# Two-layer relational graph attention on one core: which engine copies the turned W1 tiles of the pair loop out of PSUM

## The chip, the cores and the metric

The kernel runs on one core of one Trainium2 chip. The metric is the device time of one execution in microseconds (us), lower is better; a kernel's time is the median of its runs. The engines of the core work side by side, each through its own list of instructions, and meet only at semaphores: PE (TensorE, the matmuls), DVE (VectorE), ACT (ScalarE), POOL (GpSimd) and SP (SyncE, which here issues nearly all transfers).

## The reference, cut to what matters

There are 1250 nodes with 768 features and 40000 edges (source, destination, one of 3 relations). Two layers of relational graph attention follow each other, and a residual with a layer normalisation ends it:

```python
def rgat_conv(x, W, q, k, b, src, dst, etype, heads, out_ch, n_nodes):
    xr = jnp.einsum('nd,rdf->rnf', x, W)
    oi = xr[etype, dst]
    oj = xr[etype, src]
    alpha = jax.nn.leaky_relu(oi @ q + oj @ k, 0.2)
    m = jax.ops.segment_max(alpha, dst, num_segments=n_nodes)
    e = jnp.exp(alpha - m[dst])
    z = jax.ops.segment_sum(e, dst, num_segments=n_nodes)
    a = e / (z[dst] + 1e-16)
    msg = (a[:, :, None] * oj.reshape(-1, heads, out_ch)).reshape(-1, heads * out_ch)
    return jax.ops.segment_sum(msg, dst, num_segments=n_nodes) + b
h = jax.nn.elu(rgat_conv(x, W1, q1, k1, b1, ...))      # 4 heads of 192
y = rgat_conv(h, W2, q2, k2, b2, ...)                  # 1 head of 768
out = layernorm(x + y)
```

All that the change touches belongs to the first layer. There the kernel computes W1 times q1 and W1 times k1 ahead of time (so that the attention terms come out of the same matmul as x times W1), and for that it needs each 128-row tile of W1 turned.

## The kernel before, in words

**The stages.** The work begins with the edges: they are packed into codes, sorted by destination already, and gathered into windows of 6 destination nodes. From these the kernel builds `Ct`, a matrix of edge counts (source by relation and destination). The build is the **pair loop**: 106 pairs of windows. For each pair PE makes four bf16 matmuls of one-hot matrices (L1036) into PSUM bank 0 or 1, in turn; ACT copies the bank to `Ct` as 16-bit integers (L689). The one-hot matrices of two pairs, a **quad**, are made by DVE in two comparisons (L1265), one for the sources (128x1024) and one for relation and window (128x1440). There are 53 quads and two buffers, so quad q may be built only when pair 2q-3 has left PE, and pairs 2q and 2q+1 need it.

PE and ACT are tied by the two PSUM banks: pair p waits for the copy of pair p-2 (`c_ready`), and the copy of pair p waits for its matmuls (`c_done`).

**W1 inside the pair loop.** W1 has 3 relations of 6 row tiles, 18 tiles. The first 10 are handled ahead of the loop. The other 8 (tile i = 10 to 17) are put between the pairs by the table `WT_AT = {0: 10, 3: 11, 6: 12, ..., 21: 17}`: after the matmuls of pair p PE turns the tile with six transposes (L913) into two PSUM banks (`wt_tr`). The two banks are then copied, 128x384 fp32 each, to the buffer `WT[i % 2]` in SBUF, in `wt_out` (L639, on ACT; `wt_ready`). Three pairs later (`WQ_AT = {3: 10, 6: 11, ..., 24: 17}`) PE multiplies the copied tile with q1 and k1 (`wq_product`, L930, `wq_done`). In ACT's list `wt_out` of the tile turned at pair p stands behind the copy of pair p+1. At the end of a relation ACT copies the products to SBUF (`wq_out`, L623), and PE then turns and sums them (L942); within the loop this happens for relation 1 around pairs 6 to 12 and for relation 2 at pairs 24 and 25. The load of a later W1 slot (`load_w` on SP, L435) and POOL's four small memsets wait for `wq_done` too.

**After pair 27** the product x times W1, first half (L959), is put between the pairs in small portions; the loop ends with pair 105. Behind it PE goes on with L959, while ACT makes masks and DVE walks through the segment maxima (L1319). Then follow the attention of layer 1 (L1132 on PE, L1376 and L1380 on DVE), the product with W2 (L984) and the attention of layer 2 (L1174).

The order of the work on each engine is written out in its own function, and the loops over pairs (L686 on ACT, L1029 on PE) and quads (L1257 on DVE) advance side by side only through the semaphores named.

Of the kernel before, what the change touches and what calls it, by code (L numbers as in the profile page):

```python
# [36 lines left out]
def rgat(nc, x, src, dst, etype, W1, q1, k1, b1, W2, q2, k2, b2, out):  # L37
# [15 lines left out]
    HF = F // 2  # L53
# [38 lines left out]
    with ExitStack() as ctx:  # L92
# [3 lines left out]
        def sem(name):  # L96
            return ctx.enter_context(nc.semaphore(name))
# [42 lines left out]
        ps = [ctx.enter_context(nc.psum_tensor(f"ps{i}", [P, 512], F32)) for i in range(8)]  # L140
# [52 lines left out]
        WT = [bb[:, i * F:(i + 1) * F] for i in range(2)]  # L193
# [95 lines left out]
        S = {n: sem(n) for n in names}  # L289
# [45 lines left out]
        WT_AT = {3 * (i - PRE): i for i in range(PRE, R * KT)}  # L335
# [8 lines left out]
        def steps0(pair):  # L344

            n = PAIRS - T_AT
            return range(max(0, NK0 * (pair - T_AT) // n), max(0, NK0 * (pair + 1 - T_AT) // n))
# [27 lines left out]
        def wt_bank(i):  # L375

            return 4 if i % 2 == 0 else 2
# [232 lines left out]
        def _(act):  # L610
# [6 lines left out]
            def wq_out(i):  # L617

                r, kt = i // KT, i % KT
                if kt == KT - 1:  # L620
                    act.wait_ge(S["wq_done"], i + 1)
                    for b in range(2):
                        last = nc.scalar.activation(wqs[0:QP, b * HF:(b + 1) * HF], ps[6 + b][0:QP, 0:HF], copy)  # L623
                    last.then_inc(S["wqs_ready"], 1)
                if kt == 1 and r:
                    wq_columns(r - 1)

            def wq_columns(r):
                act.wait_ge(S["wq_tr"], r + 1)
                o = wqk1.rearrange("p k (a r h) -> p r k a h", a=2, r=R)[:, r]  # L630
                nc.scalar.activation(o, ps[7][:, HF:HF + KT * 2 * H].rearrange("p (k a h) -> p k a h", k=KT, a=2), copy).then_inc(S["wq_ready"], 1)

            def wt_out(i):

                act.wait_ge(S["wt_tr"], i + 1)
                if i >= 2:
                    act.wait_ge(S["wq_done"], i - 1)
                for b in range(2):
                    last = nc.scalar.activation(WT[i % 2][:, b * HF:(b + 1) * HF], ps[wt_bank(i) + b][:, 0:HF], copy)  # L639
                last.then_inc(S["wt_ready"], 1)  # L640

            def transform_out(u):
                b, t = UNITS1[u]
                if u == 0:
                    act.wait_ge(S["ones_in"], NS1)
                act.wait_ge(S["t_done"], u + 1)
                if u >= NS1:
                    act.wait_ge(xr_out[u % NS1], 16 * (u // NS1))
                o = stg1[u % NS1].rearrange("p (h c) -> p h c", h=2)[:, :, 0:HD]
                v = unit1_bank(u)  # L650
                if b == 0:
                    nc.scalar.activation(qk1t[:, t, :], v[:, HF:HF + QC], copy)
                    nc.scalar.activation(ks1[:, t, :], v[:, HF + QC // 2:HF + QC], copy, scale=SLOPE).then_inc(S["qk_ready"], 1)
                nc.scalar.activation(o, v[:, 0:HF].rearrange("p (h c) -> p h c", h=2), copy).then_inc(S["t_evac"], 1)  # L654
# [31 lines left out]
            for pair in range(PAIRS):  # L686
                act.wait_ge(S["c_done"], pair + 3)
                d = 2 * pair * WIN
                nc.scalar.activation(Ct[:, :, d:d + 2 * WIN].rearrange("p a (c b) -> p a c b", c=2),  # L689
                                     ps[pair % 2][:, 0:2 * WM].rearrange("p (c a b) -> p a c b", c=2, b=WIN), copy).then_inc(S["c_ready"], 1)  # L690
                if pair - 1 in WT_AT:
                    wt_out(WT_AT[pair - 1])
                if pair - 1 in WQ_AT:
                    wq_out(WQ_AT[pair - 1])
                if pair - 1 == WQ_END:
                    wq_columns(R - 1)
                for n in steps0(pair - 1):
                    if n % KT == KT - 1:
                        transform_out(n // KT)
# [22 lines left out]
            for _, kind, i in sorted(events):  # L722
                if kind == 0 and i >= U1 - 2:
                    if i == U1 - 2:
                        act.wait_ge(ab_in[0], 16)
                    exp_step(0, 0, i - U1 + 2)
                if kind == 0 and i == AB1_AT:
                    ab_rows(L1)
                (mask1 if kind else transform_out)(i)
# [452 lines left out]
        def _(dve):  # L1182
            V = nc.vector
            links = [0]

            def link(ins):

                links[0] += 1
                ins.then_inc(S["chain"], 1)
                dve.wait_ge(S["chain"], links[0])  # L1190
# [61 lines left out]
            for o, v in ((slo_2, slo), (mcode_2, mcode)):  # L1252
                for a in range(2):
                    last = V.tensor_copy(o[:, :, a].rearrange("p (s w t) -> p s t w", s=2, t=RUN), v.rearrange("p (s t w) -> p s t w", s=2, t=RUN))
                link(last)

            for quad in range(QUADS):  # L1257
                h, col = quad % 2, quad * 4 * RUN
                if quad >= 2:
                    dve.wait_ge(S["c_done"], 2 * quad)  # L1260
                if quad == 2:
                    dve.wait_ge(S["flag_tot"], 1)
                    V.tensor_copy(smalli[0:1, 4:5], ps[6][0:1, 511:512]).then_inc(S["flag_ready"], 1)
                for o, w, iota, codes in ((oh_s, P, i_s, slo_2), (ohm_s, WM, i_m, mcode_2)):
                    last = V.tensor_tensor(o[:, h * 4 * RUN:(h + 1) * 4 * RUN, :].rearrange("p n (b a) -> p n b a", a=2),  # L1265
                                           iota[:, :].rearrange("p (b a) -> p b a", a=2).unsqueeze(1).broadcast_to([P, 4 * RUN, w // 2, 2]),
                                           codes[:, col:col + 4 * RUN, :].unsqueeze(2).broadcast_to([P, 4 * RUN, w // 2, 2]), ALU.is_equal)
                last.then_inc(S["oh"], 1)
# [3 lines left out]
            with dve.If(held < E):  # L1272
# [7 lines left out]
                with dve.Fori(0, NW) as w:  # L1280
# [10 lines left out]
                    with dve.Fori(0, EC // 4) as j:  # L1291
                        dve.wait_ge(S["fb_c"], w * 5 + 5)
                        dve.wait_ge(S["fb_used"], w * (EC // 4) + j + 1)
                        for t in range(4):
                            V.tensor_scalar(ohs[t][0:EP, :], i_s[0:EP, :], slo_[0:EP, bass.ds(j * 4 + t, 1)], None, ALU.is_equal)
                            last = V.tensor_scalar(ohm[t][0:EP, :], i_m[0:EP, :], 1.0, mcode_[0:EP, bass.ds(j * 4 + t, 1)], ALU.add, ALU.is_equal)
# [206 lines left out]
            i = 0  # L1503
# [116 lines left out]
```

## Time and profile before

| | us |
|---|---|
| median of 3 runs (lowest 1292.36, highest 1293.78) | 1293.2 |
| the profiled execution | 1294.57 |
| its span, first to last instruction | 1292.6 |
| PE busy in the span | 1249.7 |
| DVE busy | 989.4 |
| ACT busy | 757.7 |
| pairs 0 to 25 with the eight W1 tiles, about | 41 to 66 |
| end of the pair loop, about | 138 |

Busy times say how long an engine had an instruction in work, not that it was at its peak. Where the text says that an engine waited, the profile has named the event that ended the wait. A number in brackets, as [rows 2], is a group of rows in the section below.

### The profile page before, as it was taken

How to read it: one execution, taken by the hardware profiler on the slowest of the kernel's cores; microseconds unless marked ns; L12 is line 12 of the kernel's file. 1: busy time of each engine (PE TensorE's matmuls, PEld its weight loads, DVE VectorE, ACT ScalarE, POOL GpSimd, SP SyncE). 2: the span in 40 equal slices, each digit the busy share in tenths (PEclk: the TensorE clock that was granted, in tenths of full speed). 3: DMA queues.
4: the chain of work that ended last, by engine and by line, in shares of the span. 5: the costliest groups of instructions: out<-in, count | busy, mean ns of one | idle time of the engine just before them, and what ended most of it. 6: DMA issues, size and time to landing. Idle time of an engine off the chain costs nothing.

```text
span 1292.6 us, 18743 instructions
## 1 busy us (share of the span) xinstructions
PE 1249.7 (97%) x7104; PEld 1121.7 (87%) x7104; DVE 989.4 (77%) x1289; ACT 757.7 (59%) x1210; POOL 4.9 (0%) x20
## 2 busy tenths in 40 slices
PE   6899999999999999999999999999989999999996
PEld 4766656665699999999999999999989999999995
DVE  4678899999399899999989967759844466656554
ACT  4655432332499889979979942257434444464462
POOL 1000000000000000000000000000000000000000
PEclk9999999999999999999999999999989999999998
DMA  9420131111553333323313237944486776778860
GB/s 314 164 92 31 44 122 49 50 50 43 194 122 103 103 96 103 96 68 116 118 50 99 64 109 236 313 160 159 159 307 235 248 246 204 264 261 305 283 230 34
DMA packets 93847, 195.32 MB, mean 151 GB/s; under 512 B 16125, under 2 KB 66366, under 8 KB 93762
## 3 DMA queue, kind: packets, MB, share of 16 engines
q1 hardware_dynamic: 93568, 193.77, 45.1%
q8 instruction: 57, 0.93, 0.3%
q0 software_dynamic: 96, 0.23, 0.1%
q14 instruction: 28, 0.23, 0.1%
q10 hardware_dynamic: 98, 0.16, 0.0%
HBM read 154.28 MB, written 39.85 MB: 150 GB/s over the span
## 4 chain that ended last, share of the span: by engine, by line
PE 76%; DVE 13%; ACT 4%; DMA 3%; issue 3%; SPq 1%; PEld 1%; ACTq 0%; DVEq 0%
PE ps L1174 24%; PE ps L1132 24%; PE ps L959 13%; PE ps L984 10%; DMA arena<-in_L_gnn_W 3%; DVE arena L1319 3%; PE ps L1036 3%; DVE arena L1376 2%; DVE arena L1380 2%; ACT arena L718 1%; ACT arena L719 1%; DVE ps L1448 1%; DVE misc L1329 1%; DVE arena L1461 1%; DVE arena L1398 1%
## 5 line engine op out<-in xcount | busy, mean ns | idle before, releaser
L1132 PE MATMUL ps<-arena 128*128 128x193 f32 x2400 | 396.9, 327 | 1.8 <-DVE arena L1380 1.5
L1132 PEld LDWEIGHTS ps<-arena 128*128 128x128 f32 x2400 | 392.1, 190 | 4.3 <-DVE arena L1380 3.8
L959 PE MATMUL ps<-arena,xT 128*128 128x384 f32 (+1 forms) x720 | 249.6, 494 | 0.0
L718 ACT ACTIVATE arena<-arena,misc 128x640 f32<-128x640 f32 x240 | 196.9, 820 | 31.5 <-DVE arena L1376 23.7
L959 PEld LDWEIGHTS ps<-arena,xT 128*128 128x128 f32 x720 | 131.4, 191 | 76.4 <-issue 0.3
L719 ACT ACTIVATE arena<-arena,misc 128x640 f32<-128x640 f32 x240 | 195.7, 815 | 0.0
L1376 DVE TENSOR_TENSOR arena<-arena 128x1280 f32<-128x1280 f32 x120 | 178.4, 1486 | 20.9 <-ACT arena L719 20.8
L1380 DVE SCALAR_TENSOR_TENSOR arena<-arena,Ct 128x1280 f32<-128x1280 f32 x120 | 179.2, 1493 | 15.0 <-DVE arena L1376 11.0
L1319 DVE SCALAR_TENSOR_TENSOR arena<-arena,misc 128x1250 f32<-128x1250 bf16 x108 | 155.8, 1520 | 1.5 <-ACT arena L663 1.5
L835 ACT ACTIVATE g_hi<-arena 128x512 fp32r<-128x512 f32 (+2 forms) x90 | 49.7, 552 | 158.8 <-PE ps L1174 143.6
L1174 PE MATMUL ps<-x2a,g_hi 128*128 128x384 f32 (+1 forms) x600 | 131.8, 342 | 5.2 <-issue 5.2
L1174 PE MATMUL ps<-x2b,g_hi 128*128 128x384 f32 (+1 forms) x600 | 130.2, 338 | 1.8 <-DVE g_lo L1480 1.8
L984 PE MATMUL ps<-w_hi,xt_hi 128*128 128x384 f32 (+1 forms) x360 | 122.1, 339 | 1.3 <-DVE w_lo L1427 1.3
L984 PE MATMUL ps<-w_lo,xt_hi 128*128 128x384 f32 (+1 forms) x360 | 121.4, 337 | 0.0
L984 PE MATMUL ps<-w_hi,xt_lo 128*128 128x384 f32 (+1 forms) x360 | 121.3, 337 | 0.0
L1480 DVE TENSOR_TENSOR g_lo<-arena,g_hi 128x512 fp32r<-128x512 f32 (+2 forms) x90 | 53.3, 592 | 82.4 <-ACT g_hi L835 82.1
L1174 PEld LDWEIGHTS ps<-x2a,g_hi 128*128 128x128 f32 (+1 forms) x600 | 108.3, 189 | 6.2 <-issue 5.5
L654 ACT ACTIVATE bb<-ps 128x384 f32<-128x384 f32 x60 | 29.6, 494 | 142.2 <-PE ps L959 141.2
L1174 PEld LDWEIGHTS ps<-x2b,g_hi 128*128 128x128 f32 (+1 forms) x600 | 106.5, 186 | 3.2 <-DVE g_lo L1480 2.5
L1265 DVE TENSOR_TENSOR arena<-misc,arena 128x1024 bf16<-128x1024 bf16 x106 | 78.0, 794 | 18.7 <-PE ps L1036 18.4
L793 ACT ACTIVATE stg<-ps 128x384 fp32r<-128x384 f32 x60 | 29.3, 489 | 94.5 <-PE ps L984 85.7
L1469 DVE TENSOR_TENSOR arena<-arena 128x512 f32<-128x512 f32 (+2 forms) x90 | 53.1, 590 | 40.0 <-ACT arena L828 39.9
(174 smaller groups left out, 1356.8 us busy)
## 6 DMA issues: line engine op xcount, KB each, us to landing
x2a<-xr_d SPq DMA_DIRECT2D x45, 776.0 KB, 4.3
x2b<-xr_d SPq DMA_DIRECT2D x45, 776.0 KB, 4.5
arena<-xr_d SPq DMA_DIRECT2D x120, 193.0 KB, 2.4
xr_d<-stg SPq DMA_DIRECT2D x60, 384.0 KB, 3.0
arena<-ab_d SPq DMA_DIRECT2D x12, 1280.0 KB, 6.4
xr_d<-bb SPq DMA_DIRECT2D x60, 193.0 KB, 2.2
arena<-in_L_gnn_W SPq DMA_DIRECT2D x5, 2304.0 KB, 9.8
arena<-in_L_gnn_W SPq DMA_DIRECT2D x7, 1152.0 KB, 6.8
```

What stands on the lines that cost most here:

```text
L718: nc.scalar.activation(weights1(g, r, t)[:, h, :], abr[:, r, h, :], ACT.Exp, bias=qk1t[:, t, col + R * H:col + R * H + 1])
L719: last = nc.scalar.activation(e2[t % 2][:, h, :], abr[:, r, 2 + h, :], ACT.Exp, bias=ks1[:, t, col:col + 1])
L959: last = mm(unit1_bank(u)[:, 0:w], xT[:, kt, t * P:(t + 1) * P], v, start=kt == 0, stop=kt == KT - 1)
L984: last = mm(unit_bank(u)[:, 0:w], a[:, t, kt, :], v[b % 2][:, kt, 0:w], start=kt == 0 and n == 0, stop=kt == KT - 1 and n == 2)
L1132: last = mm(bank1(g, i)[:, o:o + HD + 1], weights1(g, r, t)[:, h, i * P:(i + 1) * P], xring[t % NX][:, o:o + HD + 1], start=False, stop=Tr ...
L1174: last = mm(banks[b][0:k, 0:wide], a, xs[:, x0 + b * HF:x0 + b * HF + wide], start=j == 0 and m == 0, stop=j == RS - 1 and m == 2)
L1265: last = V.tensor_tensor(o[:, h * 4 * RUN:(h + 1) * 4 * RUN, :].rearrange("p n (b a) -> p n b a", a=2), iota[:, :].rearrange("p (b a) -> p ...
L1319: last = V.scalar_tensor_tensor(m[:, h, 0:N], cneg[i % NCN][:, 0:N], k, m[:, h, 0:N], ALU.min, ALU.max)
L1376: V.tensor_tensor(a, a, e2[t % 2], ALU.max).then_inc(S["e2_free"], 1)
L1380: V.scalar_tensor_tensor(a, a, 1.0, cc.broadcast_to([P, 2, DH]), ALU.min, ALU.mult).then_inc(S["a_ready"], 1)
L1469: link(V.tensor_tensor(v, v, g2[n % 2][:, 0:w], ALU.max))
L1480: V.tensor_tensor(g_lo[n % NG][:, 0:w], g1[n % NG][:, 0:w], g_hi[n % NG][:, 0:w], ALU.subtract).then_inc(S["a_ready"], 1)
```

## The change

The eight copies of turned W1 tiles that stand inside the pair loop leave ACT's list and go to DVE's. ACT's own copies of the ten tiles ahead of the loop stay. On DVE a tile is copied by two `tensor_copy` of 128x384 fp32, at the head of the turn of quad q, for the tile turned at pair 2q-4 or 2q-3: ahead of quads 2, 3, 5, 6, 8, 9, 11 and 12. Ahead of the copy DVE waits until the tile is turned (`wt_tr`), until the buffer's last product is done (`wq_done`) and until the tile before is there (`wt_ready`). The one-hot matrices of the quad are built behind it. Nothing else is edited.

```diff
@@ scalar: the pair loop
                 nc.scalar.activation(Ct[:, :, d:d + 2 * WIN]...).then_inc(S["c_ready"], 1)
-                if pair - 1 in WT_AT:
-                    wt_out(WT_AT[pair - 1])
                 if pair - 1 in WQ_AT:
                     wq_out(WQ_AT[pair - 1])
@@ vector: ahead of the quads
+            def wt_copy(i):
+
+                dve.wait_ge(S["wt_tr"], i + 1)
+                dve.wait_ge(S["wq_done"], i - 1)
+                dve.wait_ge(S["wt_ready"], i)
+                for b in range(2):
+                    last = V.tensor_copy(WT[i % 2][:, b * HF:(b + 1) * HF], ps[wt_bank(i) + b][:, 0:HF])
+                last.then_inc(S["wt_ready"], 1)
+
             for quad in range(QUADS):
                 h, col = quad % 2, quad * 4 * RUN
+                for p in (2 * quad - 4, 2 * quad - 3):
+                    if p in WT_AT:
+                        wt_copy(WT_AT[p])
                 if quad >= 2:
                     dve.wait_ge(S["c_done"], 2 * quad)
```

## Rows read from the trace of the kernel before

**Rows 1.** Two stretches: length, busy us by engine; last: granted clock, DMA share, GB/s

```profile
40.00:66.00 26.00, 22.76 (x287) 17.22 (x286) 17.90 (x26) 17.36 (x46) 0.20 (x4) 1.00 0.26 94
...
70.20:73.60 3.40, 3.40 (x12) 1.77 (x11) 2.12 (x3) 0.85 (x2) 0.00 (x0) 0.51 0.88 353
```

**Rows 2.** Chain of waits, pair 18 until pair 21: start us, us, what

```profile
58.60 0.47 PE ps L1036 x4
59.08 0.66 PE ps L913 x6
59.73 0.55 PE ps L930 x12
60.28 0.43 PE ps L1036 x4
60.71 0.02 issue
60.73 0.48 ACT Ct L689
61.21 0.14 issue
```

**Rows 3.** Timeline of DVE, first quads of the loop: start us, us, idle before

```profile
42.65 0.15 DVE L1263 CAST smalli<-ps 1x1 uint32<-1x1 f32 x1 [5.02 <-PE ps L1040]
42.73 4.33 DVE L1265 TENSOR_TENSOR arena<-misc,arena 128x1024 bf16<-128x1024 bf16 x6
...
51.46 1.51 DVE L1265 TENSOR_TENSOR arena<-misc,arena 128x1024 bf16<-128x1024 bf16 x2 [0.57 <-PE ps L1036]
```

**Rows 4.** Chain of waits, tile 10 turned behind pair 0, and pair 6

```profile
41.45 0.66 PE ps L913 x6
...
45.82 0.47 PE ps L1036 x4
```

**Rows 5.** Groups of instructions, for the price of a copy: busy us, mean ns | idle us before

```profile
L1239 DVE CAST arena<-ps 128x424 int32<-128x424 f32 x1 | 0.6, 600 | 11.6 <-PE ps L1019 11.6
L1229 DVE CAST arena<-arena 128x424 f32<-128x424 int32 x1 | 0.4, 381 | 0.0
L1398 DVE SCALAR_TENSOR_TENSOR arena<-ps,small,bb 128x192 f32<-128x192 f32 x40 | 13.4, 409 | 0.1
L1329 DVE TENSOR_REDUCE misc<-ps 128x4 f32<-128x512 f32 x30 | 18.9, 686 | 0.8 <-PE ps L1074 0.8
```

**Rows 6.** Timeline: a tile's ACT copies, two stalls of L930, a W1 load

```profile
48.32 0.87 ACT L639 ACTIVATE bb<-ps 128x384 f32<-128x384 f32 x2
...
50.07 0.62 PE L930 MATMUL ps<-bb,misc 128*8 128x128 f32 x12 [0.37 <-ACT arena L623]
...
64.77 0.62 PE L930 MATMUL ps<-bb,misc 128*8 128x128 f32 x12 [0.20 <-ACT bb L639]
65.44 0.37 SPq L435 DMA_DIRECT2D arena<-in_L_gnn_W  x1
```

**Rows 7.** Timeline of PE: pairs 9 and 12

```profile
48.57 0.48 PE L1036 MATMUL ps<-arena 128*128 128x180 bf16 x4 [0.34 <-ACT Ct L689]
...
51.76 0.48 PE L1036 MATMUL ps<-arena 128*128 128x180 bf16 x4 [0.34 <-ACT Ct L689]
```

**Rows 8.** Chain of waits, after pair 28, at half and at full clock

```profile
70.08 1.23 PE ps L959 x2
71.30 0.60 PE ps L1036 x4
71.90 1.43 PE ps L959 x2
...
75.88 0.31 PE ps L1036 x4
76.19 0.72 PE ps L959 x2
```

**Rows 9.** Chain of waits, behind the pair loop

```profile
138.32 70.38 PE ps L959 x218
```

## The prediction, made before the changed kernel ran

> **What bounds the kernel now.** I read the slices of the page first (PE is full nearly everywhere from pair 28 on), then the busy times of the stretch in which the eight tiles are handled, then the chain of waits through it, and last the timeline of DVE and PE there. From 40 to 66 us no engine is full: in 26 us PE is busy 22.8, DVE 17.9, ACT 17.4 [rows 1]. This is a loop of dependences, not of a full engine. The chain shows its beat, which takes three pairs: pair 18's matmuls 0.47, six transposes 0.66, the product L930 0.55, pair 19's matmuls 0.43, then ACT's copy of pair 19 with 0.02 ahead and 0.14 behind it, 0.64 together, and pair 21 follows: 2.75 us [rows 2]. The ACT copies of the tile (L639) are not in this beat. They stand behind the copy that PE waits for, and the product that needs them comes three pairs later. They are seen in the chain only where they push something else: L930 waits 0.37 us for ACT's L623, which stands behind a tile copy, and once 0.20 us for a tile copy itself [rows 6].
>
> DVE is near its limit in another way. It has room in the mean, but each quad has a start (pair 2q-3 has left PE) and a due time (pair 2q). For quads 2, 3 and 4 it runs without a gap from 42.73 for 4.33 us [rows 3]: quad 2 ends at 42.73 + 1.51 = 44.24 and quad 3, at (4.33 - 1.51)/2 = 1.41 more, at 45.65, while pair 6, the first that needs quad 3, starts at 45.82 [rows 4]. From the end of a quad to the pair that waits for it are thus at most 0.17 us. I take 0.13 for the signal. Whatever is put ahead of quad 3 lands on PE nearly in full.
>
> **The copy on DVE.** The trace has no 128x384 copy from PSUM on DVE. A cast of 128x424 from PSUM took 600 ns, one of the same size from SBUF 381 ns [rows 5]. The first is 424 columns at 0.96 GHz, 442 ns, and 158 ns fixed; the second goes at twice that pace. So 384 columns from PSUM would be 400 + 158 = 558 ns. Back to back an instruction hides a part of its duration: the 40 instructions of L1398 have a mean of 409 ns but 13.4/40 = 335 ns busy each [rows 5], 74 ns less. A tile then holds DVE for 2 x 0.484 = 0.97 us. Bounds: if a plain copy from PSUM ran as the cast from SBUF did, 381 less 40/1.92 = 360 ns, 0.29 held, 0.57 a tile. The longest row for a like amount of PSUM data is the reduction of 128x512, 686 ns [rows 5]; 0.61 held, 1.22 a tile. I take 0.97, because the PSUM cast is the same kind of operation with the same source.
>
> The Trainium skill, VectorE: DVE Perf Modes, section on the TRN2 errata, gives a copy from PSUM to SBUF 120 cycles beside its elements. By that a copy would hold DVE 504/0.96 = 525 ns, an estimate, and four tiles on the path would cost 4 x 2 x 0.04 = 0.3 us more than the sum below. No copy of this kind is in the trace; L1398, with two operands more, shows 335 ns for 192 columns where that rule would make it 325.
>
> **The first two tiles.** Tile 10 is turned at 41.45 + 0.66 = 42.11 [rows 4]. DVE, idle until 42.65 now [rows 3], copies it from 42.13 to 43.10, makes the small cast (it shifts the next by 0.08) and quad 2 from 43.18 to 44.69; pair 4 is due at 44.75 and is late by 0.07 at most. Tile 11 is turned behind pair 3 (45.82 - 2.75 = 43.07, + 0.47 + 0.66 = 44.20), so DVE need not wait for it: copy 44.6 to 45.6, quad 3 until 47.07, pair 6 at 47.20 in place of 45.82. That is **+1.38 us**.
>
> **The steady beat.** Of the remaining six tiles, three (12, 14, 16) are turned at pairs 6, 12 and 18, which is pair 2q-4 of the quad that they precede, and three (13, 15, 17) at pairs 9, 15 and 21, which is pair 2q-3. For the second kind the copy can't be early: its transposes are the last thing ahead of the quad. The path from pair p to pair p+3 is then: matmuls 0.47, transposes 0.66, signal 0.02, two copies 0.97, the quad 1.51, signal 0.13, together 3.76 us, where the beat is 2.75 now. That is **+1.0** each, for tiles 15 and 17. For the first kind the quad is ready in time: copies begin 1.15 behind pair 2q-4, the quad ends at 1.15 + 0.97 + 1.51 = 3.63, and pair 2q would come at 2.75 + 0.47 + 0.66 + 0.55 = 4.43. So no cost. But DVE may still be at the quad without a tile that stands between; after a late pair 6 it makes quad 4 until 47.07 + 1.43 = 48.50, and tile 12 is turned at 47.20 + 1.13 = 48.33. It costs 0.2 out of the 0.8 of slack. The whole load says the same: three quads of 1.45 and two tiles are 6.3 us, just under the 6.5 us which two beats take then.
>
> **What comes back.** Tile 13's beat (pair 9 to pair 12) takes 51.76 - 48.57 = 3.19 us now [rows 7], because L930 waits for L623. With the tile copy off ACT, L623 begins 0.87 us earlier [rows 6] and ends ahead of the transposes. So this beat goes from 3.19 to 3.76, **+0.57**. At pair 24 the tile has long been there, and the wait of 0.20 goes [rows 6]; the product itself takes 0.62 when it starts from idle [rows 6] and 0.55 in the chain when it doesn't [rows 2], so I count **-0.25**. The third thing freed is ACT's time, 8 x 0.87 = 7.0 us, and nothing in this stretch waits for ACT except through the copy at 0.64, which stays as long as it is.
>
> The sum: 1.38 + 0.57 + 1.0 + 1.0 - 0.25 = **+3.7 us** at pair 27.
>
> **Behind it.** From pair 28 on PE is full, and from 138.32 a single piece of the chain is 70.38 us of L959 [rows 9]. DVE's maxima, which end the stage later, begin with the end of the same loop. Neither has an origin other than the pair loop, so the delay goes through in full. The load of a later W1 slot, issued at 65.44 now [rows 6] behind `wq_done`, moves by the same 3.7 us; it is of a W1 slot that L959 reads only behind 138, so it is hidden, as are POOL's memsets. SP and POOL are moved past nothing. In DVE's list behind each `wt_copy` are its quad and all later quads, and PE waits for those; that is the cost counted. If L959 had slack anywhere up to 272 us, it would be hidden; its row shows none.
>
> The profiled span would be 1292.6 + 3.7 = 1296.3. The profiled execution is 1.4 above the median of the runs; the difference is laid on the median: 1293.2 + 3.7 = **1296.9 us**. With the copy at 0.57 the late starts are 0.60, 0.6 - 0.44, 0.6, 0.6 and -0.25, +1.7: 1294.9. With 1.22 four tiles cost 0.25 each more, +4.7: 1297.9.
>
> **Rivals.**
>
> *A longer stretch at half clock.* From 70.2 to 73.6 the granted clock is 0.51, that is the 1.2 GHz level, behind the idle time at pairs 25 to 27; around it is full [rows 1]. It costs: two portions of L959 take 1.23 and 1.43 where they take 0.72, and four pair matmuls 0.60 in place of 0.31 [rows 8], 1.22 + 0.29 = 1.5 us. The change adds waits of PE of about 1 us ahead of pairs 6, 12, 18 and 24, the last just ahead of the idle time that there is. A second stretch of this kind makes +3.7 + 1.5 = +5.2: 1298.4. Against it: one such stretch is all that 40 to 74 us shows now, with waits of 0.34 in each beat. The Trainium skill, TensorE: Matmul & The Clock Gate, Part 1, says that activity releases the throttle and an idle array falls back to it. By that rule the trace agrees: the low level at 70.2 follows the longest idle time of PE in this stretch.
>
> *DVE absorbs the copies and ACT's relief is what remains.* This is the rival on the other side. DVE is idle 8.1 of the 26 us [rows 1] and the copies are 7.8. If the copies fell into those gaps, PE would gain 0.37 + 0.25: 1292.6, not slower. It decides on whether the idle time lies ahead of a tile's copy or behind it. For tiles 12, 14 and 16 it fits, for 11, 13, 15 and 17 the gap lies ahead of transposes that have not run.
>
> *The delay is given back later.* 3.7 us of delay at pair 27 vanish in a wait that was there anyway, for instance DVE's maxima against the masks of ACT at 272 us: 1293.2, unchanged. Against it, all of them count from the end of the pair loop.
>
> *The cheap copy*, at SBUF pace, 1294.9 as above; under 0.2% from before.
>
> **How the numbers follow.** Forecast (with copies between 0.8 and 1.22) 0.55, own range 1295.6 to 1298.0; longer half clock 0.23; cheap copy 0.09; given back 0.07; ACT's relief 0.06. A measurement tells 0.2%, 2.6 us, from no change: slower means above 1295.8. Slower: 0.53 of the forecast and 0.23, 0.76. Same: 0.02 + 0.09 + 0.07 and 0.02 of the relief, 0.20. Faster: 0.04. The range takes in the cheap copy and a half-clock stretch over a dear copy's half: 1294.6 to 1299.6.
>
> **What would show it.** Right: two DVE copies per tile of about 560 ns with source PSUM; pair 6 at about 47.2 us in the span; PE waiting for DVE's L1265 about 1 us ahead of pairs 6, 12, 18 and 24 and nowhere else by that much; DVE waiting for L913 ahead of tiles 13, 15 and 17; no wait of L930 for ACT; the end of the loop 3.7 us later and the distance from there to the end unchanged. Wrong: copies near 360 ns; waits of PE ahead of the other quads too, which would mean DVE is full; a second stretch at a granted clock of about 0.5 between 40 and 80; or a later stage shorter than before.

## The result, and the profile after

The changed kernel takes 1297.04 us (median of 7 runs, 1295.42 to 1298.74), the kernel before 1293.78 (7 runs beside it, 1292.36 to 1294.09). The ratio is 1.003 with a 95% interval of 1.0018 to 1.0041: slower by 2.3 to 5.3 us. The medians are 3.26 apart, with 3.7 forecast.

The stretch in which the eight tiles are handled, in the same window as in [rows 1]. Columns: length, busy us of PE, PEld, DVE, ACT and POOL with the number of instructions, granted clock, DMA share, GB/s.

```profile
40.00:66.00 26.00, 20.00 (x241) 15.38 (x239) 23.18 (x39) 11.27 (x27) 0.00 (x0) 1.00 0.25 94
```

DVE has gone from 17.9 to 23.2 of 26 us, ACT from 17.4 to 11.3, and PE has fallen from 22.8 to 20.0. Less of PE's work fits into the same time. Who waits for whom there (us in all, times, longest), for PE:

```profile
PE ps L1034 <- DVE arena L1275: 5.3, 4, 1.6
PE ps L1034 <- ACT Ct L689: 1.0, 3, 0.3
```

L1034 and L1275 are the L1036 and L1265 of before. The list of PE's matmuls shows where the four waits are (start, us, line, idle before and what ended it). The rows are pairs 4 and 5, 6, 9, 12, 15, 18, 21, 24 and 25; [rows 4 and 7] have pairs 6, 9 and 12 of before.

```profile
43.47 0.80 PE L1034 MATMUL ps<-arena 128*128 128x180 bf16 x8
45.82 0.49 PE L1034 MATMUL ps<-arena 128*128 128x180 bf16 x4 [1.55 <-DVE arena L1275]
...
48.58 0.48 PE L1034 MATMUL ps<-arena 128*128 128x180 bf16 x4 [0.34 <-ACT Ct L689]
...
52.25 0.49 PE L1034 MATMUL ps<-arena 128*128 128x180 bf16 x4 [1.25 <-DVE arena L1275]
...
56.35 0.48 PE L1034 MATMUL ps<-arena 128*128 128x180 bf16 x4 [0.34 <-ACT Ct L689]
...
60.02 0.49 PE L1034 MATMUL ps<-arena 128*128 128x180 bf16 x4 [1.25 <-DVE arena L1275]
...
62.78 0.48 PE L1034 MATMUL ps<-arena 128*128 128x180 bf16 x4 [0.34 <-ACT Ct L689]
...
66.45 0.49 PE L1034 MATMUL ps<-arena 128*128 128x180 bf16 x4 [1.25 <-DVE arena L1275]
...
67.42 0.49 PE L1034 MATMUL ps<-arena 128*128 128x180 bf16 x4
```

A beat without a DVE wait takes 2.76 us (62.78 - 60.02), as before; one with it 3.67 us (66.45 - 62.78). Every second beat is long. The chain of waits shows what fills a long one, pair 21 to pair 24, beside the short one of [rows 2]:

```profile
62.78 0.48 PE ps L1034 x4
63.26 0.67 PE ps L911 x6
63.92 0.02 issue
63.95 1.02 DVE bb L1261 x2
64.97 1.43 DVE arena L1275 x2
66.40 0.05 issue
66.45 0.49 PE ps L1034 x4
```

Matmuls, transposes, two copies, two one-hot matrices, one behind the other: neither the product L928 nor ACT's copy is on the path any more. DVE's own list shows that it waited for the transposes and not they for it, and what a copy costs:

```profile
61.30 1.01 DVE L1261 COPY bb<-ps 128x384 f32<-128x384 f32 x2
62.23 1.50 DVE L1275 TENSOR_TENSOR arena<-misc,arena 128x1024 bf16<-128x1024 bf16 x2
63.95 1.02 DVE L1261 COPY bb<-ps 128x384 f32<-128x384 f32 x2 [0.22 <-PE ps L911]
64.89 4.57 DVE L1275 TENSOR_TENSOR arena<-misc,arena 128x1024 bf16<-128x1024 bf16 x6
```

A copy lasts 549 ns in the median of the 16, and a tile shifts what follows it by 0.93 or 0.94 us (63.95 to 64.89).

**Where the time went**, counted from pair 0 so that all that runs ahead of the loop drops out:

| us after pair 0 | before | after | difference |
|---|---|---|---|
| pair 6 | 4.85 | 6.09 | +1.24 |
| pair 9 | 7.60 | 8.85 | +1.25 |
| pair 12 | 10.79 | 12.52 | +1.73 |
| pair 15 | 14.88 | 16.62 | +1.74 |
| pair 18 | 17.63 | 20.29 | +2.66 |
| pair 24 | 23.13 | 26.72 | +3.59 |
| pair 25 | 24.35 | 27.69 | +3.34 |
| end of the pair loop | 97.35 | 100.35 | +3.00 |

From there to the end are 1154.3 us before and 1154.4 after. The end of the loop is +3.00 and not +3.34 because a stretch at half clock behind pair 26 costs a little less in the profile of after than in that of before; two later profiles without such a stretch (the kernels filled with zeros, below) end the loop at 95.69 and 99.00, 3.31 apart. The profiled span itself grew by only 1.9 (1292.6 to 1294.5), because pair 0 stands at 39.73 in place of 40.97, and the clock goes with this difference. Two stretches of both kernels, before first:

```profile
33.00:37.00 4.00, 3.89 (x30) 3.58 (x30) 3.93 (x8) 1.74 (x4) 0.00 (x0) 0.62 1.03 397
...
66.00:76.00 10.00, 8.55 (x52) 5.88 (x53) 5.49 (x8) 4.24 (x11) 0.00 (x0) 0.83 0.67 236
```

```profile
33.00:37.00 4.00, 3.69 (x45) 2.89 (x46) 3.93 (x7) 2.51 (x6) 0.00 (x0) 1.00 1.03 396
66.00:76.00 10.00, 8.06 (x58) 5.61 (x59) 6.31 (x9) 3.97 (x10) 0.20 (x4) 0.83 0.65 236
```

The profiled execution of before ran a part of 33 to 37 us at the 1.2 GHz level, that of after did not. Of the eleven profiles here only this one and one other (odd tiles behind, below) show it; their pair 0 stands at 40.97 and 40.94, that of the nine others at 39.45 to 40.05. Nothing ahead of pair 0 was edited, so a comparison of the two spans would have made the change look 1.2 us cheaper than it is.

### The profile page after: what moved, and what is told of

It is laid out like the page before. It is cut to its first block, busy times and chain, and to the rows that moved or that the text cites. A ratio compares the mean times of both kernels' runs of the same rounds, so it can differ in the third digit from the quotient of the medians.

```text
span 1294.5 us, 18743 instructions
## 1 busy us (share of the span) xinstructions
PE 1246.4 (96%) x7104; PEld 1118.7 (86%) x7104; DVE 996.7 (77%) x1305; ACT 752.2 (58%) x1194; POOL 4.9 (0%) x20
## 4 chain that ended last, share of the span: by engine, by line
PE 75%; DVE 14%; ACT 4%; DMA 3%; issue 3%; SPq 1%; PEld 1%; ACTq 0%; DVEq 0%
PE ps L1172 24%; PE ps L1130 23%; PE ps L957 13%; PE ps L982 10%; DMA arena<-in_L_gnn_W 3%; DVE arena L1329 3%; PE ps L1034 2%; DVE arena L1386 2%; DVE arena L1390 2%; ACT arena L716 1%; ACT arena L717 1%; DVE ps L1458 1%; DVE misc L1339 1%; DVE arena L1471 1%; DVE arena L1408 1%
## 5 line engine op out<-in xcount | busy, mean ns | idle before, releaser
L654 ACT ACTIVATE bb<-ps 128x384 f32<-128x384 f32 x60 | 29.6, 494 | 142.4 <-PE ps L957 141.1
L1275 DVE TENSOR_TENSOR arena<-misc,arena 128x1024 bf16<-128x1024 bf16 x106 | 78.0, 794 | 14.2 <-PE ps L1034 14.1
```

## The experiments

The first measure of each is the start of pair 25 after the start of pair 0 in the profile: before 24.35, after 27.69. I had written some expectations for pair 28; where the clock falls between them pair 25 is the clean one, and what was expected for pair 28 is compared by its difference from before. At pair 28 itself the first four experiments stand at 28.83, 32.64, 31.13 and 29.79 us, where 28.5, 31.5, 29.6 and 29.7 were expected; in the first three the half clock begins ahead of pair 28, and in the fourth just at it. Edits are shown against the changed kernel unless said otherwise, and the ratio is always to the runs of the kernel before in the same batch.

**Only the even tiles on DVE** (the ones turned at pair 2q-4).

```diff
+                if i >= PRE:
+                    act.wait_ge(S["wt_ready"], i)
...
+                if pair - 1 in WT_AT and WT_AT[pair - 1] % 2 != 0:
+                    wt_out(WT_AT[pair - 1])
...
-                    if p in WT_AT:
+                    if p in WT_AT and WT_AT[p] % 2 == 0:
                         wt_copy(WT_AT[p])
```

The first two lines stand in `wt_out`: with two engines copying in turn, ACT too waits until the tile before is there.

> Tiles 10, 12, 14 and 16 are copied by VectorE, tiles 11, 13, 15 and 17 by ScalarE. Measured in the profile from the first matmul of pair 0 to the first of pair 28: 28.63 us before, 31.97 us with all eight on VectorE (+3.34). Theory A (the cost is a path: only the tile turned at pair 2q-3 pays, because its transposes are the last thing ahead of the quad): tile 10 delays quads 2 and 3 by 0.43, which pair 6 feels as +0.3; tiles 12, 14 and 16 cost nothing; the wait of L930 for L623 goes (-0.44); so -0.1, 28.5 us, and no wait of PE for L1275 above 0.1 us but the one ahead of pair 6 (about 0.3 beyond the wait for ScalarE). Theory B (VectorE's time is what is paid, evenly over the tiles, 3.34/8 = 0.42 each): +1.7, 30.3 us. Theory C (relief of ScalarE counts): below 28.0.

Measured: pair 6 at 5.15 (+0.30), pair 25 at 24.23 (-0.12). The time is 1292.15 us, ratio 1.000 (0.999 to 1.0009). Four tiles on DVE cost nothing net (+0.30 at pair 6, -0.44 at pair 12); the only wait for DVE is the one ahead of pair 6:

```profile
PE ps L1038 <- ACT Ct L691: 2.0, 6, 0.3
PE ps L944 <- ACT arena L623: 1.3, 1, 1.3
PE ps L1038 <- DVE arena L1279: 0.6, 1, 0.6
PE ps L932 <- ACT bb L641: 0.2, 1, 0.2
```

The lines L1038, L1279, L944 and L932 are the L1036, L1265, L942 and L930 of before. The wait of the product for L623 is gone. At pair 25 theory A holds to 0.02 us, and B is out.

**Only the odd tiles on DVE.** The same edit with `% 2 != 1` on ACT and `% 2 == 1` on DVE.

> The other half: tiles 11, 13, 15 and 17 on VectorE, 10, 12, 14 and 16 on ScalarE. Theory A: +0.8 at pair 6 (the 1.24 of the changed kernel less the 0.43 that tile 10 gave), +0.48 from pair 9 to pair 12, +0.92 from 15 to 18 and from 21 to 24, -0.25 at pair 25: +2.9, 31.5 us from pair 0 to pair 28, though VectorE has only half of the copies. Theory B: +1.7, 30.3 us.

Measured: pair 6 +0.92, pair 12 +1.40, pair 25 at 27.36 (+3.01); 1296.17 us, ratio 1.0027 (1.0017 to 1.0037). The same number of copies on the same engine as in the run before, and nearly the whole cost of the change:

```profile
PE ps L1038 <- DVE arena L1279: 4.6, 4, 1.3
PE ps L1038 <- ACT Ct L691: 1.0, 3, 0.3
PE ps L932 <- ACT arena L623: 0.4, 1, 0.4
```

It matters which tile is copied there, more than how many. The two halves add up to 2.89 and not to 3.34: with tile 13 on DVE the beat from pair 9 to pair 12 waits for DVE, and the 0.44 that the even tiles alone gave back there is not had.

**All eight on DVE, the odd ones behind their quad.** The position alone is changed, the instructions are those of the changed kernel.

```diff
                 for p in (2 * quad - 4, 2 * quad - 3):
-                    if p in WT_AT:
+                    if p in WT_AT and WT_AT[p] % 2 == 0:
                         wt_copy(WT_AT[p])
...
                 last.then_inc(S["oh"], 1)
+                if 2 * quad - 3 in WT_AT:
+                    wt_copy(WT_AT[2 * quad - 3])
```

> All eight tiles on VectorE as in the changed kernel, same instructions, but the tiles turned at pair 2q-3 (11, 13, 15, 17) are copied behind the one-hot matrices of quad q, not ahead of them. Theory A with VectorE's load as the floor: the path over the transposes is cut; worked through by the same durations, pair 6 +0.3, pair 12 +0.5, pair 24 +0.3, and at pair 24 the product waits about 0.4 for tile 17; in all about +1.0, 29.6 us from pair 0 to pair 28. Theory B (the load alone decides): the load is the same, so +3.3, 32.0 us.

Measured: pair 6 at 5.15, pair 12 at 11.27 (+0.48), pair 24 at 23.87 (+0.74), pair 25 at 25.35 (+1.00); 1294.18 us, ratio 1.0012 (1.0002 to 1.0022). Of 3.34 us 2.34 were the position, so theory B is out here too. What is left is DVE's load and one late product:

```profile
PE ps L1034 <- DVE arena L1275: 1.7, 4, 0.6
PE ps L1034 <- ACT Ct L689: 1.5, 4, 0.6
PE ps L928 <- DVE bb L1261: 0.4, 1, 0.4
```

Pair 24 stands at +0.74 where I had written +0.3: the 0.3 was what is added there, on top of pair 12's shift. The list of waits puts 0.59 us ahead of pair 24 to ACT, but DVE's list has two quads from 61.83 for 2.92 us, so until 64.75, and pair 24 starts at 64.81:

```profile
61.83 2.92 DVE L1275 TENSOR_TENSOR arena<-misc,arena 128x1024 bf16<-128x1024 bf16 x4
64.67 1.02 DVE L1261 COPY bb<-ps 128x384 f32<-128x384 f32 x2
```

```profile
64.81 0.49 PE L1034 MATMUL ps<-arena 128*128 128x180 bf16 x4 [0.59 <-ACT Ct L689]
```

It is DVE's load that is the floor here, as the forecast of the run has it: from 42.13 us until pair 24 has started, DVE waits once, for 0.27 us ahead of 55.70.

**Each tile half by ACT, half by DVE.** ACT copies the first 384 columns at its old place, with a semaphore of its own for PE.

```diff
+                if pair - 1 in WT_AT:
+                    i = WT_AT[pair - 1]
...
+                    nc.scalar.activation(WT[i % 2][:, 0:HF], ps[wt_bank(i)][:, 0:HF], copy).then_inc(S["wt_half"], 1)
...
-                for b in range(2):
+                for b in range(1, 2):
                     last = V.tensor_copy(WT[i % 2]...)
```

> Each of the eight tiles is copied half by VectorE (second 384 columns) and half by ScalarE (first 384 columns), each where its copy of a whole tile stood. Theory A (the path holds the copies in series): one copy less on the path, 0.46 to 0.47 us, so pair p to pair p+3 takes 3.21 in place of 3.67: +0.35 at pair 6, 0.0 from 9 to 12, +0.46 from 15 to 18 and from 21 to 24, -0.25 at pair 25: +1.0, 29.7 us. Theory D (a wait of PE for VectorE costs a fixed price by itself, whatever is copied): the steps stay near 3.67, about +3 in all.

Measured: pair 6 +0.45, pair 9 +0.47, pair 12 +0.48, pair 25 at 25.50 (+1.15); the long beats take 3.19 to 3.20 us in place of 3.67. 1293.92 us, ratio 1.0005 (0.9995 to 1.0015). One copy less shortens the path by 0.47 to 0.48, its own share; pair 6 was 0.1 dearer than I had said. Theory D is out. The lines L1043, L1284 and L949 are the L1036, L1265 and L942 of before.

```profile
PE ps L1043 <- DVE arena L1284: 3.1, 4, 0.8
PE ps L1043 <- ACT Ct L689: 1.4, 4, 0.3
PE ps L949 <- ACT arena L623: 1.3, 1, 1.3
```

**ACT's relief alone.** In the kernel without DVE copies ACT copies 8 columns of each tile at the old place. The kernel leaves out the rest of each copy, so the products read mostly old data, and its time alone is of use.

```diff
+                    nc.scalar.activation(WT[i % 2][:, 0:8], ps[wt_bank(i)][:, 0:8], copy).then_inc(S["wt_ready"], 1)
...
-                for p in (2 * quad - 4, 2 * quad - 3):
-                    if p in WT_AT:
-                        wt_copy(WT_AT[p])
```

> ScalarE's relief without VectorE's copies. The eight tiles are not copied: in place of each ScalarE copies 8 columns at the same place in its list, so that the products in the loop read mostly old data (work left out, time only). Theory A: PE waited for ScalarE's tile copies only at the product of tile 12 (0.37 and 0.07 of restart) and of tile 17 (0.20 and 0.05), so pair 25 starts 0.7 us after pair 0 earlier than before, at 23.7 in place of 24.35, and the time falls by 0.7, hardly to be told. Theory C (ScalarE is what the stretch turns on): each of the eight beats gets shorter by some of the 0.87 us of a tile copy, 2 to 6 us in all.

Measured: pair 25 at 23.65, so 0.70 us is all that ACT's relief can bring up to there, and theory C is out. The time was 1292.79 us, ratio 0.9994 (0.9983 to 1.0005), with its runs 6.7 us apart.

**The clock: the kernel before, with PE kept busy in two waits.** The edit is against the kernel before.

```diff
                 elif kt == 0:
+                    if r == 1:
+                        for _ in range(6):
+                            mm(ps[5][:, 0:512], zm[:, 0:P], zm[:, 0:512], start=True, stop=True)
                     pe.wait_ge(*landed(r))
...
                 if pair == WQ_END:
+                    for _ in range(5):
+                        mm(ps[4][:, 0:512], zm[:, 0:P], zm[:, 0:512], start=True, stop=True)
                     wq_transposes(R - 1)
```

> The kernel before, with ScalarE's copies as they were, and matmuls of zeros into unused banks in two places in which PE waits: six of 512 columns ahead of the wait for the second W1 slot (PE idle from 31.4 to 33.1 us) and five behind pair 25, ahead of the sums of relation 2 (1.31 us). They add work that nobody reads. Theory A: the stretches at half clock (32.6 to 36.0 in some executions, 70.2 to 73.6) follow these waits; with PE busy in them the granted clock stays at 1.00, and the time falls by 1.5 us for the second and by 1.2 more in executions which had the first: 1291.2 or a little under, against 1292.7. Theory E (the clock falls for another reason, or zeros do not count as work): the stretches stay, and the time is as before or longer by the added matmuls.

Measured: 1291.24 us, ratio 0.9981 (0.9971 to 0.999). The two windows of above, 33 to 37 and 66 to 76 us:

```profile
33.00:37.00 4.00, 3.69 (x37) 2.89 (x38) 3.93 (x7) 2.27 (x6) 0.00 (x0) 1.00 1.03 396
66.00:76.00 10.00, 9.52 (x69) 6.94 (x70) 6.68 (x10) 4.56 (x12) 0.00 (x0) 1.00 0.61 230
```

Up to pair 28 nothing moved (28.64 against 28.63 us), and the loop ended at 95.69 in place of 97.35: the stretch at half clock costs 1.66 us here. The median is 2.3 us below that of the kernel before in the same batch (1293.57), where 1.5, or 2.7 in executions with both stretches, were expected. Theory A fits this profile; a second one of the same program, below, does not bear it out in full.

**A combined version.** Tiles 12, 14 and 16 on DVE, `WQ_END` one pair later, and the zeros in both waits (six and three).

```diff
-        WQ_END = max(WQ_AT) + 1
-        T_AT = WQ_END + 2
+        ON_DVE = (12, 14, 16)
+        WQ_END = max(WQ_AT) + 2
+        T_AT = WQ_END + 1
```

> A version that should beat both: only the tiles 12, 14 and 16 are copied by VectorE (the ones that wait for nothing), all others by ScalarE; the sums of relation 2 are put behind pair 26 in place of pair 25, so that one pair's matmuls fill a part of the wait; and matmuls of zeros fill the wait for the second W1 slot (six) and what is left of the wait ahead of the sums (three). Theory A: pair 25 at 23.9 us after pair 0 in place of 24.35; the first L959 at 28.1 in place of 28.95; no stretch at half clock, 1.5 more; together -2.4 us, about 1290.3 against 1292.7. If VectorE's load mattered for any tile (theory B), three tiles would cost 1.3 and pair 25 would stand above 25.

Measured: pair 25 at 23.91 as expected, end of the loop at 95.03, the clock at 1.00 in both stretches. 1290.99 us, ratio 0.9987 (0.9978 to 0.9996). It is 2.6 us below the kernel before in the same batch (1293.57), with 2.4 expected; the 1290.3 that I had written counts from an earlier batch, in which the kernel before took 1292.7. Most of it comes with the zeros: its 0.25 from the filled kernel before is less than either set of runs is wide. Moving three tiles brings 0.4 us at pair 25 and nothing that a time can show.

**Before and after, both filled, on one chip.**

> The kernel before with matmuls of zeros in two waits of PE, once more, beside the next one on the same chip: about 2.0 us under the kernel before, with a spread of its runs under that of the kernel before, and no stretch at half clock between 30 and 80 us.

> The changed kernel, all eight tiles on VectorE, with the same matmuls of zeros in the same two waits. If the changed kernel costs 3.3 us by its path alone and the clock is no part of it, it stands 3.3 us above the kernel before with the same matmuls, and its pair 25 starts 27.7 us after pair 0, as in the changed kernel. If the added waits of about 1.2 us ahead of pairs 6, 12, 18 and 24 bring the clock down too, a stretch at half clock shows in 40 to 80 us in spite of the zeros, and the distance is larger than 3.3.

Measured: 1291.07 us (1289.22 to 1293.07) and 1294.71 us (1293.85 to 1296.58), 3.6 us apart. Pair 25 stands at 24.37 and 27.67, pair 28 at 28.65 and 31.96: +3.31. The expectation on the clock was right for the changed kernel and wrong for the other. The filled kernel before, the same program as above, now had a stretch at half clock in its profiled execution, and the changed one had none, in spite of four waits of 1.25 to 1.54:

```profile
66.00:76.00 10.00, 9.64 (x59) 6.51 (x59) 5.48 (x9) 3.65 (x9) 0.00 (x0) 0.83 0.60 226
```

```profile
66.00:76.00 10.00, 9.27 (x75) 6.26 (x76) 7.03 (x11) 4.87 (x12) 0.20 (x4) 1.00 0.67 236
```

(In the second kernel's row POOL's four memsets fall into the stretch too.) In this window all seven profiles without zeros have the half clock, and of the four with zeros one has it. So the zeros make it rarer, as far as eleven profiles can tell, and they don't rule it out.

## Why the prediction was right, step by step

**What bounds the stretch.** It said a loop of dependences, with room on DVE in the mean and none ahead of a due quad. The even and the odd tiles show it: four copies each, -0.12 and +3.01 us.

**The first two tiles**, +1.38 forecast, +1.24 measured. From the end of the quad to PE's matmul are 0.05 us (row "issue" ahead of pair 24), where I took 0.13 from the gap of 0.17 in [rows 3, 4]. Tile 10's part, 0.30, and tile 11's, 0.92, were seen apart in the runs with the even and with the odd tiles.

**The steady beat**, 3.76 forecast, 3.67 measured; 0.08 of the difference is the signal again. So +0.92 for tiles 15 and 17 each, forecast 1.0, and 0 for tiles 12, 14 and 16 as forecast.

**The copy**, 558 ns and 0.97 us for a tile forecast, 549 ns and 0.93 measured. The PSUM cast of [rows 5] was the right neighbour. The Trainium skill's figure (VectorE: DVE Perf Modes, the section on the TRN2 errata) would hold DVE 525 ns for each copy, an estimate; the trace shows half of 0.93, 0.47 us, so the measurement decides against it here. As a duration from start to end it lies nearer, 525 against 549 ns. The prediction's price for dear copies was not added up like its price for cheap ones: tiles 10 and 11 both lie ahead of pair 6, so at 1.22 us a tile five tiles would have cost 0.25 more each and not four, +4.95 in place of +4.7. The measured 0.93 made this of no account.

**What comes back.** Tile 13's beat +0.57 forecast, +0.48 measured; pair 24 to 25 -0.25 and -0.25. ACT's relief alone is worth 0.70 up to pair 25, which bounds the rival on the other side: DVE cannot absorb the odd tiles' copies, since its gap lies ahead of their transposes.

**Behind it.** The distance from the end of the loop to the end changed by about 0.1 us. That agreement is in part luck: two profiles of one program, the filled kernel before, have 1154.24 and 1152.19 us there: the second ran only half as long at half clock near 957 us (granted clock 0.89 in place of 0.79 over 952 to 968 us). Before and after both show 0.79 there. So nothing was given back at a like clock, and the medians, 3.26 and 3.64 us apart, agree. Three numbers that I had named did not come as written. Pair 6 was to stand at 47.2 us in the span and stands at 45.82: 1.24 us of this is the shorter part ahead of the loop, and 0.14 the term of the first two tiles. The end of the loop was to come 3.7 us later and came 3.00 later counted from pair 0. The span was to be 1296.3 and was 1294.5. The median, forecast 1296.9 and measured 1297.04, is closer than the terms are: the kernel before came out at 1293.78 in its seven runs and not at the 1293.2 of three, which made up for the 0.4 by which the sum was too high.

**The rival of a longer half clock** (0.23) did not show in the two profiles of kernels with all eight copies ahead of their quads, but it is not absent. A stretch twice as long as that of before (granted clock 0.66 or 0.67 over 66 to 76 us in place of 0.83) was seen in three profiles: with the odd tiles on DVE, with them behind, and with ACT's relief alone, in which PE waited for DVE not once from 40 to 66 us. In those three the loop ends 74.02 to 74.24 us after pair 25, in the ones with the shorter stretch 72.58 to 73.01, in those with none 71.12 to 71.33. The long stretch thus comes without any wait for DVE; whether such waits make it more frequent is not shown, with one or two profiles of a kernel. What goes with it is where the stretch begins: 1.4 to 2.4 us behind the start of pair 25 in the three long ones, 3.1 to 4.9 in the five short ones. The length of an idle time alone does not decide: in the changed kernel PE sat idle for 1.55 us ahead of pair 6, longer than the 1.31 after which the level fell before, and the granted clock stayed at 1.00 from 40 to 66 us. What does decide isn't settled: the same program showed no stretch and a short one. For the difference of the medians it stays a possible part of what lies between 3.3 and 3.6 us.

The sum: forecast +3.7 at pair 27, measured +3.34 at pairs 25 and 28, and +3.3 in the medians. The terms that were off by a little are pair 6 (0.14), tile 13's beat (0.09) and the two steady beats (0.08 each), together 0.4, and all of one sign: the signal and, by a little, the copy were priced too high.

## What to carry to other kernels

Ask of a moved operation not how full its new engine is but when its input is ready against the due time of what stands behind it in that engine's list. A copy whose input is made by the last work ahead of a deadline costs its whole length there, even on an engine that idles a third of the time; one whose input lies ready early costs little or nothing as long as the engine's load fits (here 0 for tiles 12, 14 and 16, and 0.30 for tile 10, which stood ahead of two quads without slack). Try the other side of the neighbour (here: behind the quad, 2.34 of 3.34 us back) before another engine.

## What the runs showed of the hardware

- A copy of 128x384 fp32 from PSUM took 549 ns on VectorE and held it for 0.47 us; on ScalarE it took 488 ns. From the start of the first to the end of the second, two took 1.01 or 1.02 us on VectorE and 0.87 on ScalarE [rows 6]. ScalarE is the faster one on this size, by 0.15 us a tile.
- From the end of VectorE's instruction in the profile to the start of PE's matmul that waited for it were 0.05 us (changed kernel, ahead of pair 24), from the end of ScalarE's 0.14 [rows 2].
- The granted clock fell to its 1.2 GHz level in one execution of a program and not in another from 66 to 76 us, and near 957 us it stayed there for a shorter or a longer time. From 33 to 37 us it fell in two of eleven profiles, in kernels that before this place are alike but for the zeros. Pair 0 stood about 1 us later with the fall at the first place (40.94 and 40.97 against 39.45 to 40.05); at the second it cost 1.2 to 1.7 us, or 2.7 to 2.9 where it was long; at the third two profiles of one program differ by 2.05. These are sizes like the spread between the runs of a kernel (1.7 us in 7 runs of the kernel before, 4.9 in 31), but no run beside the profiled ones shows its clock by place, so what the spread comes from is not shown. Counting from pair 0 to pair 25 kept all three out.
